# A softmax over a graph's adjacency on one core: the exp's tail in two halves, and the sums two units behind the cosines instead of three

## The reference

```python
def _L0_gnn_ref(t, x, adj, alpha, beta):
    deg = jnp.clip(adj.sum(axis=1), 1.0)
    dis = deg ** (-0.5)
    adj_norm = dis[:, None] * adj * dis[None, :]
    diffusion = adj_norm @ x - x
    norms = jnp.maximum(jnp.linalg.norm(x, axis=-1), COS_EPS)
    sim = x @ x.T / (norms[:, None] * norms[None, :])
    attn = jax.nn.softmax(beta * sim * adj, axis=1)
    return diffusion + jax.nn.sigmoid(alpha) * (attn @ x - x)
h = jnp.maximum(_layernorm(x, axis=-1), 0.0)
x = x + _L0_gnn_ref(L0_gnn_t, h, adj, L0_gnn_alpha, L0_gnn_beta)
```

## Time and profile before

| | us |
|---|---|
| median of 3 timed runs | 1921.21 (1920.76 to 1921.44) |
| the profiled execution, its own time | 1921.04 |
| its span, from the first to the last instruction | 1919.1 |
| TensorE busy | 1827.4 (95%) |
| VectorE busy | 1226.5 (64%) |
| ScalarE busy | 1306.8 (68%) |
| GpSimd busy | 1269.1 (66%) |

### The profile page before, as it was taken

One profiled execution on the slowest core, in us unless ns is written; L12 is line 12 of the kernel. 1 busy time (PEld: TensorE's weight loads), 2 busy tenths in 40 slices (PEclk: granted clock), 3 DMA queues, 4 the chain that ended last, 5 costly groups with the idle time before them and its releaser, 6 DMA issues.

```text
span 1919.1 us, 44747 instructions
## 1 busy us (share of the span) xinstructions
PE 1827.4 (95%) x19602; PEld 1408.7 (73%) x19602; DVE 1226.5 (64%) x1382; ACT 1306.8 (68%) x1262; POOL 1269.1 (66%) x792
## 2 busy tenths in 40 slices
PE   0489999999999999999999999999998999999998
PEld 0366777777777777777777777777777888888887
DVE  6887787787778778777877877787775210111111
ACT  7688898889889888988988898899887000000000
POOL 3099999999999999999999999999883000000000
PEclk9699999999999999999999999999999999999999
DMA  9639887767888877778888767888426755554530
GB/s 177 97 63 135 106 106 101 100 89 102 100 106 101 108 105 89 100 96 100 106 100 109 100 89 100 100 107 100 116 92 239 226 178 182 170 200 165 202 107 12
DMA packets 188455, 229.38 MB, mean 120 GB/s; under 512 B 9316, under 2 KB 164964, under 8 KB 183396
## 3 DMA queue, kind: packets, MB, share of 16 engines
q0 software_dynamic: 135168, 67.13, 45.1%
q1 hardware_dynamic: 25060, 144.71, 20.6%
q10 hardware_dynamic: 28032, 14.69, 3.0%
HBM read 352.32 MB, written 75.50 MB: 223 GB/s over the span
## 4 chain that ended last, share of the span: by engine, by line
PE 93%; ACT 3%; DVE 2%; issue 1%; POOL 1%; DMA 0%; SPq 0%; DVEq 0%; ACTq 0%
PE cos_ps L670 34%; PE top_ps L700 12%; PE top_ps L704 12%; PE cos_ps L726 12%; PE top_ps L726 12%; PE top_ps L702 12%; ACT arena L329 1%; ACT xe L353 0%; POOL hlo L278 0%; POOL ustage L287 0%; PE cos_ps L656 0%; DMA asb<-x_in 0%; DVE ustage L518 0%; DVE ptmp L489 0%; ACT xe L337 0%
## 5 line engine op out<-in xcount | busy, mean ns | idle before, releaser
L287 POOL TENSOR_TENSOR ustage<-xe,ustage 128x1024 f16<-128x1024 f32 x512 | 1094.7, 2142 | 155.3 <-ACT xe L410 148.2
L584 DVE TENSOR_TENSOR xe<-cos_ps,arena 128x1024 f32<-128x1024 f32 x512 | 627.0, 1225 | 286.2 <-PE cos_ps L670 191.5
L406 ACT ACTIVATE ustage<-xe,ebias,ab 128x1024 f16<-128x1024 f32 x512 | 635.3, 1241 | 132.2 <-DVE xe L584 128.8
L700 PE MATMUL top_ps<-h,ustage 128*128 128x129 f16 x4096 | 719.2, 220 | 6.2 <-POOL ustage L287 6.1
L704 PE MATMUL top_ps<-h,ustage 128*128 128x129 f16 x4096 | 718.9, 220 | 0.0
L702 PE MATMUL top_ps<-hlo,ustage 128*128 128x128 f16 x4096 | 718.4, 219 | 0.0
L410 ACT ACTIVATE xe<-xe,ebias,ab 128x1024 f32<-128x1024 f32 x512 | 628.6, 1228 | 5.5 <-POOL ustage L287 4.7
L700 PEld LDWEIGHTS top_ps<-h,ustage 128*128 128x128 f16 x4096 | 400.8, 98 | 75.6 <-POOL ustage L287 15.9
L702 PEld LDWEIGHTS top_ps<-hlo,ustage 128*128 128x128 f16 x4096 | 400.8, 98 | 56.6
L704 PEld LDWEIGHTS top_ps<-h,ustage 128*128 128x128 f16 x4096 | 400.8, 98 | 0.0
L559 DVE TENSOR_REDUCE top_ps<-arena 128x8 f32<-128x1024 uint16 x256 | 311.8, 1218 | 2.0 <-DMA arena<-adj_in_dram 2.0
(11 more groups left out here) (87 smaller groups left out, 1017.5 us busy)
## 6 DMA issues: line engine op xcount, KB each, us to landing
arena<-adj_in_dram POOLq DMA_DIRECT2D x256, 256.0 KB, 8.6
at_scratch<-arena SPq DMA_DIRECT2D x128, 512.0 KB, 3.3
arena<-at_scratch SPq DMA_DIRECT2D x26, 2048.0 KB, 8.9
xe<-at_scratch SPq DMA_DIRECT2D x6, 2048.0 KB, 8.5
h_scratch<-arena SPq DMA_DIRECT2D x4, 1024.0 KB, 7.6
arena<-h_scratch SPq DMA_DIRECT2D x2, 2048.0 KB, 8.8
ustage<-h_scratch ACTq DMA_DIRECT2D x16, 256.0 KB, 3.0
ptmp<-x_in ACTq DMA_DIRECT2D x64, 64.0 KB, 5.0
```

Of the source, the lines that this page charges most:

```text
L287: nc.gpsimd.tensor_tensor(elo[:, n % ES, :], ef[:, n % XS, :], ehi[:, n % ES, :], ALU.subtract).then_inc(elo_done, 1)
L406: nc.scalar.activation(ehi[:, n % ES, :], xm[:, n % XS, :], ACT.Exp, bias=ebias[:, 0:1], scale=ab[:, 1:2]).then_inc(ehi_done, 1)
L584: nc.vector.tensor_tensor(xm[:, n % XS, :], cos_ps[:, n % 2, :], at8[:, m % W, :, n % B], ALU.mult).then_inc(x_done, 1)
L700: nc.tensor.matmul(top_ps[:, bank, col:col + P + 1], head, h1[:, s, 0:P + 1], start=(first and t % 3 == 0), stop=final, skip_group_check=True)
```

## The change

The constant LAG goes from 3 to 2. GpSimd's tail of a unit becomes two instructions of 128 x 512, each of which counts `elo_done` up by one; every wait on `elo_done` is rewritten for two counts a unit. In `sums` there are now two waits, one ahead of tile 0 for the first half and one ahead of tile 4 for the second.

```diff
-    LAG = 3
+    LAG = 2
...
-                    sp.wait_ge(elo_done, UNITS)
+                    sp.wait_ge(elo_done, 2 * UNITS)
...
-                nc.gpsimd.tensor_tensor(elo[:, n % ES, :], ef[:, n % XS, :], ehi[:, n % ES, :], ALU.subtract).then_inc(elo_done, 1)
+                for half in range(2):
+                    of = slice(HALF * half, HALF * (half + 1))
+                    nc.gpsimd.tensor_tensor(elo[:, n % ES, of], ef[:, n % XS, of], ehi[:, n % ES, of], ALU.subtract).then_inc(elo_done, 1)
...
-                    act.wait_ge(elo_done, n - XS + 1)
+                    act.wait_ge(elo_done, 2 * (n - XS + 1))
...
-                pe.wait_ge(elo_done, n + 1)
                 if n < TILES and n % 4 == 0:
                     pe.wait_ge(hlo_ready, n // 4 + 1)
                 for t in range(PT):
+                    if t % 4 == 0:
+                        pe.wait_ge(elo_done, 2 * n + t // 4 + 1)
```

## The result

The changed kernel takes 2016.78 us (median of 4 runs, 2016.04 to 2018.07), the kernel before 1921.33 beside it: a ratio of 1.050 [1.049, 1.051], 95.5 us slower. The forecast was 1992 us, +71, in a range of 1964 to 2028. The direction came out as forecast, and so did the mechanism inside the loop. The size was 25 us short: the time lies inside the whole range, but outside the inner band of 1975 to 2012 that had most of the chance.

What follows compares the result with a forecast made beforehand. PE was taken as the bound, busy 95% of the span and never waiting in the main loop. Chain 44, load units 20, panel ends 7, tails of h 0.6, earlier start -1.0: +71 us, 1992 us, range 1964 to 2028.

Steps and rivals of the forecast that it cites:

- PE could only lose: Main loop, 205 to 1445 us: PE waits for nobody, so the change can only add a wait; slower was given 0.94.
- The chain: One unit's cosines to those three units later: 8.20 us, 2.73 a unit against 2.645, +44 us over 500 units.
- The load units of GpSimd: Units where GpSimd also issues a load of rows: 2.84 us of GpSimd each, 240 such units, +20 us.
- The start of the loop: First sums of the loop: they may start one half earlier, giving back 1.0 us.
- So the clock costs nothing in my sum: PE's short idles in nearly every unit: granted clock stays 1.00, as from 110 to 120 us before, adding 0.
- The panel ends: Accumulator copies ahead of ScalarE's head at 7 panel ends: about 1.1 us late, less 0.13 already paid, +7 us.
- rival B: Mid-stream handoff in the sums costs more than 0.06 us, or the clock oscillates: 2017 to 2037 us; chance 0.14.
- Rival A: Main loop: only one of two bounds bites, chain or GpSimd's loads: +47 to +51, 1968 to 1972 us; chance 0.14.
- C: Sums: PE gets its first half no earlier than the second; chain 8.88 us, +157, 2078 us; chance 0.04.
- D: Main loop: no difference, since signals overlap more than the starts show; 1921 us; chance 0.03.
- E: Ends of the loop: half-unit earlier starts give back 1.0 and 1.7 us, loop costs nothing; 1918.5 us; chance 0.03.
- three signs: Main loop: waits in nearly every unit, units 2.73 us apart without loads; a clock under 1.00 inside would show it wrong.

## Why the prediction was right, and where it was off

- That PE could only lose, since it never waited in the loop: right. No experiment was measurably faster than the kernel before.
- The chain, 5.26 + 1.08 + 1.12 + 0.06 + 0.68 = 8.20 us over three units: the mechanism was right and shown by moving the cut (8.10 expected, 8.13 measured) and by taking the cut away (8.82 expected and measured). The term "1.08 + 1.12 (two halves)" was mis-sized: it measured 1.11 + 1.16, and the chain 8.29. In the 270 or so units without a load, 0.03 us each are 8 us.
- The load units of GpSimd, "2.16 + 0.69, I take 2.84": right in kind, 2.90 in fact, by the same halves. 0.06 x 240 = 14 us. The two corrections are 22 us.
- The start of the loop: "the first sums may start one half earlier, -1.0" was wrong. The sums do start earlier, but the cosines of unit 3 now stand behind them and PE's idle time ahead of them is longer; with the clock's fall the start cost +3.6 us. "So the clock costs nothing in my sum" holds for the loop but not for its start, where it is about 1.5 us.
- The panel ends: +1.0 each forecast, net of the 0.13 that each cost before. Measured against the neighbours they cost 0.89, which is 0.76 net, or 5.3 us for the seven instead of 7.
- The second wait in mid-stream costs 0.05 to 0.06 us, as at the head of the sums, so the mechanism of rival B is out, though the measured time lies at the lower edge of the 2017 to 2037 us that it was priced at. The granted clock stayed at 1.00 from 205 to 1445 us with PE's weight loads waiting 312 times, mostly for 0.26 us each. So the oscillation that the Trainium skill reports for frequent micro-idles (TensorE: Matmul & The Clock Gate, on PSUM-queue depth-cycling) did not come in this stretch.
- Rival A is out (both bounds bite), C is out by the chain of 8.29 us against its 8.88 and by the whole tail's +155, D and E by the result.
- Of what I said would show it was right, three signs came otherwise. Waits stood in 266 of 437 units and not in nearly every one. I looked for plain units of 2.73 each; they are 2.65, 2.74 and 2.90 in turn. And a granted clock under 1.00 inside the loop, named as a sign of being wrong, came at its start.

Set side by side, in us, from the two profiled executions (unit numbers are those of the cosines that begin and end a stretch):

| part | forecast | measured |
|---|---|---|
| start of the loop, units 0 to 4 | -1.0 | +3.6 |
| units 4 to 12, with tails of h | +0.6 | +2.0 |
| chain and loads, units 12 to 511 | +64 | +85.8 |
| seven panel ends | +7 | +5.3 |
| before and behind the loop | 0 | -0.6 |
| sum | +71 | +96.1 |

The 22 us of the halves' length are nearly the whole error. The other errors are 4.6, 1.4, -1.7 and -0.6 us and partly cancel.

The main error came from one choice of row. I took the length of a half from an instruction of the same width and types but with an operand in another form. The whole tail's row could not have corrected it: 2.14 with 1.12 gives a fixed part of 0.10 us, 2.14 with 1.163 gives 0.18, and both are possible. The trace of before has no row of 128x512 in the tail's own form, so the honest forecast would have carried both lengths. At 3 and 4% of a GpSimd instruction, times 1024 of them with no slack, it was a quarter of the loss.

## What to carry to other kernels

When the lag between two places of one engine's list is cut, add up the whole chain from one iteration's first stage to the first stage of the iteration that it holds up, divide by the number of iterations between the two (here the lag plus one: three), and compare it with the bound engine's period; what counts is the piece that is ready last together with all the work that stands behind its wait. Where the chain comes within a few per cent of the period, its share of every hundredth of a microsecond of a step (here a third) is paid in every unit, and an engine that is overloaded only now and then becomes a bound too. Before signalling in pieces, see whether the work can be put in another order, so that what needs no late input goes first: that (with the loads spread) took the same lag from +155 to +23 us, with the tail in one piece. What spreading the loads alone gives with a whole tail, no run shows. Ask also what PE has left to do while it waits for the first input of all: a shorter lag leaves it less.

## What the runs showed of the hardware

GpSimd's subtraction of fp32 and fp16 to fp16 took 2.142 us for 1024 elements per partition, 1.163 for 512 and 0.667 for 256. With the fp16 operand in runs of 128 at a step of 130 elements, 512 took 1.124 us, shorter than without any gaps; with all three operands in runs of 128 at a step of 256 it took 1.162. Neither swapping two of the buffers nor numbers 16384 times smaller changed the 1.16.

TensorE's granted clock stayed at 1.00 through 1240 us with 312 waits of mostly 0.26 us each. It fell to 0.50 for about 3 us behind an idle time of 3.60 us at the start of the loop; there the small matmuls started 0.11 us apart instead of 0.056.
